# Scores of the first 128 keys in three high/low passes, with their parts in free slots of the gated outputs

## The chip, the cores and the metric

The kernel runs on one NeuronCore of a Trainium2 chip. TensorE multiplies matrices into the eight banks of PSUM; VectorE, ScalarE (called ACT in the profile) and GpSimd (POOL) work beside it; the DMA transfers are issued from SyncE (SP). Each engine works through its own instructions in order, and they hand over to each other by semaphores. The metric is the device time of one execution in microseconds, the median of the runs.

## The reference

One decoder layer on x of 4 batches, 256 tokens and 256 channels, in float32: gated linear attention with a decay in 16 heads of 128, then attention over a context, then a layer of 16 routed and 2 shared experts. The change touches the first part alone:

```python
q, k = silu(conv(h @ Wq)), silu(conv(h @ Wk))      # causal convolution of 4 taps
q, k = layernorm(q) * qn_w + qn_b, layernorm(k) * kn_w + kn_b   # per head of 128
for t in range(256):                               # for each batch and head
    S = (1 - beta[t]) * S + beta[t] * outer(v[t], k[t])
    o[t] = S @ q[t]
x = x + (o * silu(h @ Wg)) @ Wo
```

The kernel computes the recurrence of a head as a masked product: for each batch, the scores k q^T of all pairs of tokens, times a matrix of decays, times beta v.

## The kernel before

All of x stays in SBUF, 1024 tokens in 8 tiles of 128. The transposed, normalised input is kept twice, as a high part (xT_hi, in the reduced type fp32r) and a low part (xT_lo, what is left). A product in three passes, mm3 (L1344 to L1348), adds high by low, low by high and high by high, each a matmul on fp32r data; mm (L1341) is one matmul on plain float32.

The attention is a pipeline over the 16 heads. step(g, k) handles head 4g + k on each engine, and beside it the early parts of heads k + 1 and k + 2. The order is written out by hand in each engine's step. What follows is the order in TensorE's step (L1582 to L1618) before the change:

- values_unit twice (values of a later pair of heads, two units of 12 mm3 passes);
- to_features(0) to (3) (L1479): transposes of the normalised q (chunks 0, 1) and k (chunks 2, 3), with project_out of an earlier pair of heads and the gate's projection, project_in(k+1, 2, ...), between them;
- to_tokens(k+1) in four chunks (L1465): transposes after the convolution. Between them stand the q projection of head k + 2 in chunks 0 and 1 (project_in what = 0, L1445) and the scores;
- scores(g, k, b) for the batches b = 0 to 3 (L1490): two plain matmuls, the first 128 keys by all 256 queries (L1497), and the other 128 keys by the last 128 queries (L1498);
- outputs(0), the k projection of head k + 2 in two chunks (what = 1), outputs(1). The chunk u of q and k waits for taps_done, the taps of chunk u - 2, since it reuses the bank that they read (L1455).

ACT's step (L754 to L785) holds: normalise (L661) of four chunks, affine (L675), which drains the transposes with the norm's weight and bias into qk, gates (L642), silu (L655), first_taps (L625) of head k + 2, gated_high (L686), the high part of the outputs of the head before, and high, the high part of the weights. POOL's step (L491 to L507) holds the low parts: gated_low (L461), split_low for the weights, low_values or low_projection, and last_tap (L453), the last tap of the convolution. VectorE's step (L1132 to L1162) holds: the norm's factors (L1055), gated_out (L1087), taps (L1062, L1070), the scan of the decays (L1036, L1042), add_unit, head_stats (L1045, L1051) of head k + 1, and decayed (L1078, L1084), scores times decay, for each batch as it comes. Its order from the scores on: decayed(0), decayed(1), head_stats(2), decayed(2), taps(k+2, 0), decayed(3), head_stats(3), taps(k+2, 1), gated_out(0).

The scores go through two banks (c_ring); t_drained counts ACT's drains, c_drained VectorE's. gated_hi and gated_lo have four slots of 1024 columns, one for each head of a group. Head 15 is written out on its own (ACT L795 to L800, TensorE L1628 to L1648), heads 14 and 15 have no head k + 2.

Of the kernel before, what the change touches and what calls it, by code (L numbers as in the profile page):

```python
# [25 lines left out]
P = 128  # L26
# [4 lines left out]
N = 512  # L31
# [95 lines left out]
def decoder_layer(nc, x_in, ctx_in, xw_in, xb_in, wb_in, bb_in, w_in, prm_in, wv_in, wo_in,  # L127
# [5 lines left out]
    with ctx:  # L133
# [104 lines left out]

        bank = [ctx.enter_context(nc.psum_tensor(f"bank{i}", [P, N], F32)) for i in range(8)]
# [21 lines left out]
        t_full, t_drained = sem("t_full"), sem("t_drained")  # L261
        c_full, c_drained = sem("c_full"), sem("c_drained")
# [173 lines left out]
        def _(pool):  # L436
# [40 lines left out]
            split_low(0, 1)  # L477
            last_tap(0, 0, range(2 * NCH))
# [12 lines left out]
            def step(g, k):  # L491

                pool.wait_ge(rstd_ready, units(g, k, 1, 1))
                if has(g, k - 1):
                    gated_low(*head(g, k - 1), 0)
                if has(g, k + 1):
                    last_tap(*head(g, k + 1), (1,))
                    last_tap(*head(g, k + 1), (2,))
                low_shared(g, k)
                if has(g, k + 1):  # L500
                    last_tap(*head(g, k + 1), (3,))
                if has(g, k - 1):
                    gated_low(*head(g, k - 1), 1)
                if has(g, k + 2):
                    last_tap(*head(g, k + 2), (0,))
                if has(g, k + 1):
                    split_low(*head(g, k + 3))  # L507
# [72 lines left out]
        def _(act):  # L580
# [104 lines left out]

            def gated_high(g, k, c):  # L686
# [67 lines left out]
            def step(g, k):  # L754
# [8 lines left out]
                affine(g, k, (1,))  # L763
                if has(g, k + 1):
                    silu(*head(g, k + 1), (1,))
                    gates(*head(g, k + 1), (1,))
                affine(g, k, (2,))
                affine(g, k, (3,))
                if has(g, k + 1):
# [28 lines left out]
            affine(g, k, range(2 * NCH))  # L798
# [541 lines left out]
        def _(pe):  # L1340
# [149 lines left out]
            def scores(g, k, some):  # L1490

                for b in some:

                    pe.wait_ge(t_drained, units(g, k, 8, 7 + b // BPC))
                    pe.wait_ge(c_drained, c_scores(g, k) + (b - 1))
                    q0, k0 = b * L, T + b * L
                    mm(c_ring[b % 2][:, 0:L], qk[:, k0:k0 + P], qk[:, q0:q0 + L], True, True)  # L1497
# [84 lines left out]
            def step(g, k):  # L1582
# [19 lines left out]
                if has(g, k + 1):  # L1602
                    to_tokens(*head(g, k + 1), (1,))
                scores(g, k, (0,))
# [4 lines left out]
                if has(g, k + 2):  # L1609
                    project_in(*head(g, k + 2), 0, (1,))  # L1610
                scores(g, k, (3,))
                if has(g, k + 1):
                    to_tokens(*head(g, k + 1), (3,))
                outputs(g, k, (0,))
# [218 lines left out]
```

## Time and profile before

| | |
|---|---|
| median of 3 runs | 578.58 us (578.08 to 578.64) |
| the profiled execution | 578.73 us |
| its span | 576.9 us |
| busy in the span | TensorE 96%, its weight loads 84%, VectorE 75%, ACT 69%, POOL 51% |
| granted TensorE clock | 0.997 of full speed |
| attention | to about 400 us; heads 2 to 13 take 22.9 us each |

The page lists the busy time of each engine, the waits with what ended them, and the chain of work that ended last. The timeline gives, for each instruction or merged run of equal instructions, the start, the time from the first start to the last end, the engine, the line, the operation with its operands and, in brackets, the idle time of the engine before it with what ended it. The start of the next row is often before the end of the one above, as instructions are pipelined. A plain float32 matmul shows as two records.

### The profile page before, as it was taken

To read this page: it belongs to the slowest core of one execution; us is meant where nothing else is said; L and a number is where in the kernel's file an instruction comes from. 1 tells how busy PE (TensorE), PEld (TensorE's weight loads), DVE (VectorE), ACT (ScalarE), POOL (GpSimd) and SP (SyncE) were. 2 spreads that over 40 slices of the span, in tenths; PEclk is the share of its full clock that TensorE was granted. 3 is DMA by queue.
4 is the path that set the end of the run, shared out by engine and by line. 5 is a ranking of instruction groups with operands and counts; after the bars stand their busy time and mean duration, and the time that the engine had idled before them with its cause. 6 is when DMAs were issued, how large, how long until landed. Compare 5 with 4: busy or idle time off the path is not lost.

```text
span 576.9 us, 9944 instructions
## 1 busy us (share of the span) xinstructions
PE 554.7 (96%) x3392; PEld 485.0 (84%) x3392; DVE 432.5 (75%) x1046; ACT 398.1 (69%) x782; POOL 292.7 (51%) x194
## 2 busy tenths in 40 slices
PE   4898999999999999999999999989899999999997
PEld 1597889989989999899899898878678888888887
DVE  8769989998998899889989998978956543323333
ACT  3979988979779789798797887786653334333431
POOL 2335756746666457366565673420021565556552
PEclk9999999999999999999999999999999999999999
DMA  6132032032030130230211202210020433233321
GB/s 201 31 120 84 0 120 84 1 119 83 3 120 25 59 120 2 82 107 15 84 51 70 83 1 102 82 30 2 1 56 5 164 129 98 95 129 127 94 81 73
DMA packets 18001, 42.31 MB, mean 73 GB/s; under 512 B 4736, under 2 KB 6528, under 8 KB 17952
## 3 DMA queue, kind: packets, MB, share of 16 engines
q1 hardware_dynamic: 17952, 41.69, 21.6%
q8 instruction: 27, 0.44, 0.3%
q14 instruction: 22, 0.18, 0.1%
HBM read 40.47 MB, written 1.21 MB: 72 GB/s over the span
## 4 chain that ended last, share of the span: by engine, by line
PE 85%; DVE 7%; ACT 4%; issue 1%; DMA 1%; SPq 1%; DVEq 0%; ACTq 0%
PE bank L1346 21%; PE bank L1348 20%; PE bank L1347 20%; PE bank L1342 14%; PE bank L1486 5%; PE bank L1474 4%; ACT tok L671 2%; DMA w_raw<-in_w 1%; DVE stats L1051 1%; DVE xT_lo L986 1%; DVE stats L971 1%; DVE x L1187 1%; ACT values L585 1%; DVE x L1336 0%; DVE raw L1070 0%
## 5 line engine op out<-in xcount | busy, mean ns | idle before, releaser
L1346 PE MATMUL bank<-xT_lo,w_hi 128*128 128x512 f32 x320 | 133.7, 418 | 1.9 <-DVE conv L1070 1.2
L1348 PE MATMUL bank<-xT_hi,w_hi 128*128 128x512 f32 x320 | 125.9, 394 | 0.0
L1347 PE MATMUL bank<-xT_hi,w_lo 128*128 128x512 f32 x320 | 125.3, 392 | 0.0
L464 POOL TENSOR_TENSOR gated_lo<-gated,gated_hi 128x512 fp32r<-128x512 f32 x30 | 38.8, 1293 | 116.5 <-ACT gated_hi L691 112.8
L671 ACT ACTIVATE tok<-bank,nmr,rstd 128x128 f32<-128x128 f32 x256 | 91.2, 503 | 2.0 <-DVE nmr L966 2.0
L1346 PEld LDWEIGHTS bank<-xT_lo,w_hi 128*128 128x128 f32 x320 | 60.5, 189 | 16.3 <-DVE conv L1070 3.2
L459 POOL TENSOR_TENSOR raw<-tap,raw 128x506 f32<-128x506 f32 x32 | 62.0, 1936 | 20.3 <-DVE raw L1070 16.3
L459 POOL TENSOR_TENSOR conv<-tap,conv 128x506 f32<-128x506 f32 x32 | 62.0, 1936 | 20.1 <-DVE conv L1070 20.1
L1348 PEld LDWEIGHTS bank<-xT_hi,w_hi 128*128 128x128 f32 x320 | 60.2, 188 | 13.6
L1347 PEld LDWEIGHTS bank<-xT_hi,w_lo 128*128 128x128 f32 x320 | 60.7, 190 | 9.1
L1051 DVE BATCH_NORM_STATS2 stats<-bank 128x6 f32<-128x128 f32 x256 | 56.4, 284 | 14.8 <-PE bank L1474 14.8
L1042 DVE TENSOR_TENSOR_SCAN decay<-obet,dmask 128x1536 f32<-128x1536 f32 x16 | 62.0, 3873 | 0.0
L1226 DVE TENSOR_TENSOR conv<-bank,tok 128x512 f32<-128x512 f32 x36 | 24.8, 690 | 44.2 <-PE bank L1348 44.0
L1234 DVE TENSOR_TENSOR gated_lo<-gate,gated_hi 128x512 fp32r<-128x512 f32 x32 | 24.0, 785 | 39.6 <-ACT gated_hi L849 39.6
L546 POOL TENSOR_TENSOR gate<-conv,tap 128x512 f32<-128x512 f32 x32 | 42.5, 1332 | 21.4 <-DVE conv L1226 13.2
L849 ACT ACTIVATE gated_hi<-gate 128x512 fp32r<-128x512 f32 x32 | 18.9, 628 | 48.0 <-PE bank L1348 41.0
L683 ACT ACTIVATE qk<-bank,prm 128x512 f32<-128x512 f32 x64 | 51.5, 844 | 0.0
L1070 DVE SCALAR_TENSOR_TENSOR raw<-bank,prm,raw 128x510 f32<-128x510 f32 x64 | 46.8, 743 | 5.6 <-ACT tap L639 4.5
L1342 PE MATMUL bank<-qk 128*128 128x256 f32 (+1 forms) x256 | 50.2, 329 | 0.5 <-DVE x L1103 0.3
L1070 DVE SCALAR_TENSOR_TENSOR conv<-bank,prm,conv 128x510 f32<-128x510 f32 x64 | 46.8, 743 | 3.4 <-ACT tap L639 2.3
L1342 PEld LDWEIGHTS bank<-qk 128*128 128x128 f32 x256 | 43.2, 190 | 5.7 <-issue 0.7
L1342 PE MATMUL bank<-probs,values 128*128 128x256 f32 (+1 forms) x256 | 47.0, 327 | 0.0
(184 smaller groups left out, 1398.4 us busy)
## 6 DMA issues: line engine op xcount, KB each, us to landing
obet<-obet_rows SPq DMA_DIRECT2D x16, 768.0 KB, 4.3
w_raw<-in_w SPq DMA_DIRECT2D x22, 384.0 KB, 4.8
tap<-route_rows SPq DMA_DIRECT2D x16, 512.0 KB, 4.0
w_raw<-in_w SPq DMA_DIRECT2D x12, 256.0 KB, 3.0
wv_raw<-in_wv SPq DMA_DIRECT2D x8, 256.0 KB, 4.8
wo_raw<-in_wo SPq DMA_DIRECT2D x8, 256.0 KB, 4.9
w_raw<-in_w SPq DMA_DIRECT2D x12, 128.0 KB, 2.1
x<-in_x SPq DMA_DIRECT2D x2, 512.0 KB, 4.7
```

The costliest lines, as they stand in the source:

```text
L459: nc.gpsimd.tensor_tensor(y, r, y, ALU.add).then_inc(conv_done, 1)
L464: nc.gpsimd.tensor_tensor(gated_lo[:, cc], gated[:, c * N:(c + 1) * N], gated_hi[:, cc].bitcast(F32), ALU.subtract).then_inc(gated_lo_read ...
L546: nc.gpsimd.tensor_tensor(weighted(m, c), prod[:, two(m, c)], wbc[:, s * T + c * N:s * T + (c + 1) * N], ALU.mult).then_inc(e_weighted, 1)
L671: ins = nc.scalar.activation(tok[:, t * P:(t + 1) * P], t_ring[u][:, i * P:(i + 1) * P], ACT.Identity, scale=rstd[:, t:t + 1], bias=nmr[:, ...
L683: nc.scalar.activation(qk[:, u * N:(u + 1) * N], t_ring[u][:, :], ACT.Identity, scale=prm[:, o:o + 1], bias=prm[:, o + 1:o + 2]).then_inc( ...
L1042: nc.vector.tensor_tensor_scan(decay[:, :], obet[:, :], dmask[:, :], 0.0, ALU.mult, ALU.add).then_inc(decay_ready, 1)
L1051: ins = nc.vector.bn_stats(stats[:, 6 * t:6 * t + 6], t_ring[u][:, i * P:(i + 1) * P])
L1070: ins = nc.vector.scalar_tensor_tensor(out=y, in0=r, scalar=prm[:, o + 3 - back:o + 4 - back], in1=y, op0=ALU.mult, op1=ALU.add)
L1342: return nc.tensor.matmul(o, l, r, start=start, stop=stop)
L1346: nc.tensor.matmul(o, l_hi, r_lo, start=start, stop=False, skip_group_check=loose)
L1347: nc.tensor.matmul(o, l_lo, r_hi, start=False, stop=False, skip_group_check=loose)
L1348: return nc.tensor.matmul(o, l_hi, r_hi, start=False, stop=stop, skip_group_check=loose)
```

## The change

In the scores, the product of the first 128 keys with the 256 queries is taken in three passes over high and low parts (mm3), where it was one plain product. The product of the other 128 keys stays. The parts are made for each head: split_q (1024 columns of q, in slot k of gated_hi and gated_lo) and split_k (the first 128 keys of each batch, 512 columns, in slot k + 1). ACT makes the high parts (high_q(0) after affine(1); high_k and high_q(1) after affine(3)), POOL the low ones (low_q(0), low_k, low_q(1) after last_tap(3)). The scores wait for k_lo_ready and q_lo_ready instead of t_drained. In TensorE's step the second q chunk of head k + 2 moves from between scores(2) and scores(3) to ahead of scores(0), and to_tokens(3) moves ahead of scores(3).

```diff
@@ -236,6 +236,15 @@
             return (wv_hi[:, 64:64 + 3 * D], wv_lo[:, 64:64 + 3 * D]) if n == 3 else (
                 wo_hi[:, 0:3 * D], wo_lo[:, 0:3 * D])
 
+        def split_q(hi, k):
+            return (gated_hi if hi else gated_lo)[:, k % G * T:(k % G + 1) * T]
+
+        def split_k(hi, k):
+            o = (k + 1) % G * T
+            return (gated_hi if hi else gated_lo)[:, o:o + N]
+
         bank = [ctx.enter_context(nc.psum_tensor(f"bank{i}", [P, N], F32)) for i in range(8)]
         a_ring, t_ring, c_ring = bank[0:2], bank[2:6], bank[6:8]
         e_ring, y_acc = bank[0:4], bank[4:8]
@@ -259,6 +268,8 @@
         ld_route = [sem(f"ld_route{i}") for i in range(2)]
         a_full, a_copied, gate_drained = sem("a_full"), sem("a_copied"), sem("gate_drained")
         t_full, t_drained = sem("t_full"), sem("t_drained")
+        q_hi_ready, k_hi_ready = sem("q_hi_ready"), sem("k_hi_ready")
+        q_lo_ready, k_lo_ready = sem("q_lo_ready"), sem("k_lo_ready")
         c_full, c_drained = sem("c_full"), sem("c_drained")
         w_hi_ready, w_lo_ready = sem("w_hi_ready"), sem("w_lo_ready")
         wv_hi_ready, wv_lo_ready = sem("wv_hi_ready"), sem("wv_lo_ready")
@@ -475,6 +486,20 @@
             split_low(0, 0)
             low_values(0, 0)
             split_low(0, 1)
+
+            def low_q(g, k, u):
+                pool.wait_ge(q_hi_ready, units(g, k, NCH, u + 1))
+                nc.gpsimd.tensor_tensor(split_q(False, k)[:, u * N:(u + 1) * N], qk[:, u * N:(u + 1) * N],
+                                        split_q(True, k)[:, u * N:(u + 1) * N].bitcast(F32),
+                                        ALU.subtract).then_inc(q_lo_ready, 1)
+
+            def low_k(g, k):
+                pool.wait_ge(k_hi_ready, units(g, k, 1, 1))
+                nc.gpsimd.tensor_tensor(
+                    split_k(False, k).rearrange("p (b t) -> p b t", b=B),
+                    qk[:, T:2 * T].rearrange("p (b t) -> p b t", b=B)[:, :, 0:P],
+                    split_k(True, k).bitcast(F32).rearrange("p (b t) -> p b t", b=B),
+                    ALU.subtract).then_inc(k_lo_ready, 1)
             last_tap(0, 0, range(2 * NCH))
 
             def low_shared(g, k):
@@ -499,6 +524,9 @@
                 low_shared(g, k)
                 if has(g, k + 1):
                     last_tap(*head(g, k + 1), (3,))
+                low_q(g, k, 0)
+                low_k(g, k)
+                low_q(g, k, 1)
                 if has(g, k - 1):
                     gated_low(*head(g, k - 1), 1)
                 if has(g, k + 2):
@@ -682,6 +710,17 @@
                         act.wait_ge(c_full, c_scores(g, k - 1) + B)
                     nc.scalar.activation(qk[:, u * N:(u + 1) * N], t_ring[u][:, :], ACT.Identity,
                                          scale=prm[:, o:o + 1], bias=prm[:, o + 1:o + 2]).then_inc(t_drained, 1)
+
+            def high_q(g, k, u):
+                act.wait_ge(t_drained, units(g, k, 8, 4 + u + 1))
+                nc.scalar.activation(split_q(True, k)[:, u * N:(u + 1) * N], qk[:, u * N:(u + 1) * N],
+                                     ACT.Copy).then_inc(q_hi_ready, 1)
+
+            def high_k(g, k):
+                act.wait_ge(t_drained, units(g, k, 8, 8))
+                nc.scalar.activation(split_k(True, k).rearrange("p (b t) -> p b t", b=B),
+                                     qk[:, T:2 * T].rearrange("p (b t) -> p b t", b=B)[:, :, 0:P],
+                                     ACT.Copy).then_inc(k_hi_ready, 1)
 
             def gated_high(g, k, c):
 
@@ -761,11 +800,14 @@
                 if has(g, k + 1):
                     gates(*head(g, k + 1), (0,))
                 affine(g, k, (1,))
+                high_q(g, k, 0)
                 if has(g, k + 1):
                     silu(*head(g, k + 1), (1,))
                     gates(*head(g, k + 1), (1,))
                 affine(g, k, (2,))
                 affine(g, k, (3,))
+                high_k(g, k)
+                high_q(g, k, 1)
                 if has(g, k + 1):
                     silu(*head(g, k + 1), (2,))
                     silu(*head(g, k + 1), (3,))
@@ -795,7 +837,11 @@
             g, k = NG - 1, 3
             shared_high(g, k)
             normalise(g, k, range(2 * NCH))
-            affine(g, k, range(2 * NCH))
+            affine(g, k, (0, 1))
+            high_q(g, k, 0)
+            affine(g, k, (2, 3))
+            high_k(g, k)
+            high_q(g, k, 1)
             gated_high(g, k - 1, 1)
             context_exp(range(G))
 
@@ -1491,10 +1537,13 @@
 
                 for b in some:
 
-                    pe.wait_ge(t_drained, units(g, k, 8, 7 + b // BPC))
+                    pe.wait_ge(k_lo_ready, units(g, k, 1, 1))
+                    pe.wait_ge(q_lo_ready, units(g, k, NCH, 1 + b // BPC))
                     pe.wait_ge(c_drained, c_scores(g, k) + (b - 1))
                     q0, k0 = b * L, T + b * L
-                    mm(c_ring[b % 2][:, 0:L], qk[:, k0:k0 + P], qk[:, q0:q0 + L], True, True)
+                    kk, qq = slice(b * P, (b + 1) * P), slice(q0, q0 + L)
+                    mm3(c_ring[b % 2][:, 0:L], split_k(True, k)[:, kk], split_k(False, k)[:, kk],
+                        split_q(True, k)[:, qq], split_q(False, k)[:, qq], True, True)
                     mm(c_ring[b % 2][:, L:DW], qk[:, k0 + P:k0 + L], qk[:, q0 + P:q0 + L],
                        True, True).then_inc(c_full, 1)
 
@@ -1601,16 +1650,16 @@
                     project_in(*head(g, k + 2), 0, (0,))
                 if has(g, k + 1):
                     to_tokens(*head(g, k + 1), (1,))
+                if has(g, k + 2):
+                    project_in(*head(g, k + 2), 0, (1,))
                 scores(g, k, (0,))
                 scores(g, k, (1,))
                 if has(g, k + 1):
                     to_tokens(*head(g, k + 1), (2,))
                 scores(g, k, (2,))
-                if has(g, k + 2):
-                    project_in(*head(g, k + 2), 0, (1,))
+                if has(g, k + 1):
+                    to_tokens(*head(g, k + 1), (3,))
                 scores(g, k, (3,))
-                if has(g, k + 1):
-                    to_tokens(*head(g, k + 1), (3,))
                 outputs(g, k, (0,))
                 if has(g, k + 2):
                     project_in(*head(g, k + 2), 1, (0,))
```

## Rows read from the trace of the kernel before

**Rows 1.** The page's busy time, share of the span and instructions of each engine.

```profile
PE 554.7 (96%) x3392; PEld 485.0 (84%) x3392; DVE 432.5 (75%) x1046; ACT 398.1 (69%) x782; POOL 292.7 (51%) x194
```

**Rows 2.** Busy time by stretches; columns as in the first row.

```profile
core 0: us, PE busy (x) PEld busy (x) DVE busy (x) ACT busy (x) POOL busy (x), PEclk, DMA share, GB/s
92.00:346.00 254.00, 254.00 (x1645) 229.21 (x1644) 228.28 (x541) 212.43 (x422) 153.43 (x89) 1.00 0.19 63
```

**Rows 3.** Waits, 100 to 340 us: engine, line, releaser; total us, times, longest.

```profile
PEld bank L1346 <- DVE conv L1070: 1.5, 6, 0.3
...
PEld bank L1346 <- DVE raw L1070: 1.3, 5, 0.3
```

**Rows 4.** Timeline of TensorE in one head, and the next head's to_features(3).

```profile
205.06 0.28 PE L1346 MATMUL bank<-wo_lo,gated_hi 128*128 128x256 f32 x1
...
206.49 0.60 PE L1486 MATMUL bank<-ident,tok 128*128 128x128 f32 x4
...
208.32 0.60 PE L1486 MATMUL bank<-ident,tok 128*128 128x128 f32 x4
208.76 0.60 PE L1474 MATMUL bank<-ident,conv 128*128 128x128 f32 x4
...
210.58 0.60 PE L1474 MATMUL bank<-ident,conv 128*128 128x128 f32 x4
211.01 1.47 PE L1342 MATMUL bank<-qk 128*128 128x256 f32 x8
212.32 0.60 PE L1474 MATMUL bank<-ident,conv 128*128 128x128 f32 x4
...
218.62 0.47 PE L1346 MATMUL bank<-xT_lo,w_hi 128*128 128x512 f32 x1
...
231.18 0.60 PE L1486 MATMUL bank<-ident,tok 128*128 128x128 f32 x4
```

**Rows 5.** Timeline of VectorE in the same head: scan, statistics, first products, last taps.

```profile
204.21 3.87 DVE L1042 TENSOR_TENSOR_SCAN decay<-obet,dmask 128x1536 f32<-128x1536 f32 x1
...
211.21 0.89 DVE L1051 BATCH_NORM_STATS2 stats<-bank 128x6 f32<-128x128 f32 x4 [0.33 <-PE bank L1474]
212.02 1.13 DVE L1084 TENSOR_TENSOR probs<-bank,decay 128x384 f32<-128x384 f32 x2
...
217.02 1.52 DVE L1070 SCALAR_TENSOR_TENSOR raw<-bank,prm,raw 128x510 f32<-128x510 f32 x2
218.46 0.68 DVE L1095 TENSOR_TENSOR gated<-bank,gate 128x512 f32<-128x512 f32 x1
```

**Rows 6.** Timeline of ACT in the same head: gates(1), affines, gated_high, next first tap.

```profile
208.52 0.60 ACT L652 ACTIVATE gate<-bank 128x512 f32<-128x512 f32 x1 [0.73 <-PE bank L1348]
209.01 1.45 ACT L683 ACTIVATE qk<-bank,prm 128x512 f32<-128x512 f32 x2
...
212.62 0.64 ACT L691 ACTIVATE gated_hi<-gated 128x512 fp32r<-128x512 f32 x1
215.07 0.78 ACT L637 ACTIVATE raw<-bank,prm 128x512 f32<-128x512 f32 x1 [1.81 <-issue]
```

**Rows 7.** Timeline of POOL in the same head: last_tap(3) and gated_low.

```profile
204.83 4.32 POOL L459 TENSOR_TENSOR conv<-tap,conv 128x506 f32<-128x506 f32 x1
213.34 1.30 POOL L464 TENSOR_TENSOR gated_lo<-gated,gated_hi 128x512 fp32r<-128x512 f32 x1 [4.20 <-ACT gated_hi L691]
```

**Rows 8.** Timeline of head 0: ACT's last two affines and VectorE's first products.

```profile
51.74 1.57 ACT L683 ACTIVATE qk<-bank,prm 128x512 f32<-128x512 f32 x2
...
53.80 1.13 DVE L1084 TENSOR_TENSOR probs<-bank,decay 128x384 f32<-128x384 f32 x2
```

**Rows 9.** Timeline of head 14: the same two places.

```profile
369.20 1.44 ACT L683 ACTIVATE qk<-bank,prm 128x512 f32<-128x512 f32 x2
...
371.78 1.00 DVE L1084 TENSOR_TENSOR probs<-bank,decay 128x384 f32<-128x384 f32 x2
```

**Rows 10.** Timeline of head 15: affines, scores, and VectorE's wait for them.

```profile
384.49 2.88 ACT L683 ACTIVATE qk<-bank,prm 128x512 f32<-128x512 f32 x4
...
387.01 1.47 PE L1342 MATMUL bank<-qk 128*128 128x256 f32 x8
...
387.93 1.14 DVE L1084 TENSOR_TENSOR probs<-bank,decay 128x384 f32<-128x384 f32 x2 [2.02 <-PE bank L1342]
```

More of the change, by code:

```diff
@@ L1608, in step @@
                 scores(g, k, (2,))
-                if has(g, k + 2):
-                    project_in(*head(g, k + 2), 0, (1,))
-                scores(g, k, (3,))
                 if has(g, k + 1):
                     to_tokens(*head(g, k + 1), (3,))
+                scores(g, k, (3,))
                 outputs(g, k, (0,))
```

## The prediction

> **What bounds the kernel now.** I read the page's busy shares first: TensorE is busy in 96% of the span [rows 1]. By stages it is more pointed: from 92 to 346 us, some eleven heads of the attention, TensorE is busy for 254.00 of 254.00 us at a granted clock of 1.00 [rows 2]. That looks as if only TensorE's work counted. The waits of that stage say more. Weight loads of a projection (L1346) wait for VectorE's taps (L1070), once in each head: 6 + 5 times, 2.8 us in all [rows 3]. TensorE's busy share hides this, because a matmul's modelled end reaches over a short pause. So two loops close at the same moment in each head: TensorE's own work, and a loop that goes from TensorE through VectorE's queue back to TensorE.
>
> I follow one head (step k = 2 of the third group) through four engines. to_features(3) starts on TensorE at 208.32 us [rows 4]; I call this X. The same row comes 22.86 us later in the next head, at 231.18 [rows 4]. The scores start at 211.01 (X + 2.69). VectorE starts its first product of scores and decay at 212.02, right after its statistics (211.21, 0.89 us), and from there on works without a pause: four products, two groups of statistics, two pairs of taps; the second pair starts at 217.02 (1.52 us) and ends at 218.54, and the next instruction follows at 218.46 in overlap [rows 5]. The projection chunk that needs this second pair starts on TensorE at 218.62 [rows 4], 0.08 us after it. VectorE has no slack between 212.02 and 218.54: 6.52 us of back-to-back work. Whatever delays its first product delays that chunk, and all that comes after it in TensorE's order, by as much.
>
> **The change, part by part.**
>
> Scores on TensorE. A batch now costs half of 212.32 − 211.01 = 1.31 us, 0.655 us [rows 4]. Twelve high/low matmuls of 256 columns take 206.49 − 205.06 = 1.43 us, 0.119 us each [rows 4]. The 128-column product stays; the plain 256 and 128 columns share 0.655 us as 2 to 1, so it is 0.218 us and the one replaced 0.437. New batch: 3 × 0.119 + 0.218 = 0.575 us. Gain 0.08 us, for 64 batches 5.1 us. Changes between the two kinds of matmul have no clean row; between −0.02 and +0.09 us a batch, I take 0.01.
>
> ACT gets three copies of 512 columns a head. Nearest row: gated_high (L691), 0.64 us, with some 0.52 us to the next start [rows 6]. high_q(0) stands before silu(1) and gates(1). ACT waits 0.73 us ahead of gates(1) for TensorE [rows 6], so its 0.52 us is covered; without that cover it costs 0.52 us. Then gates(1) at 208.52, the affines of both halves of the key at 209.01, ended 1.45 us later at 210.46 [rows 6]. high_k waits for the last of these: 210.50 to 211.13. high_q(1) follows to 211.65, and silu(2), silu(3) and the first taps come 1.1 us later than now. That is inside the 1.81 us that ACT waits ahead of its next first tap at 215.07 [rows 6], and it must wait less there, since the moved chunk is done sooner.
>
> POOL gets three subtractions of 512 columns; nearest row gated_low (L464), 1.30 us [rows 7]. last_tap(3) starts at 204.83 and takes 4.32 us, to 209.15 [rows 7], as it lies beside VectorE's scan (204.21, 3.87 us) [rows 5]. low_q(0) runs 209.15 to 210.45; low_k can only start after high_k, at 211.21 (gated_low follows its copy by 0.08 us: 212.62 + 0.64 against 213.34 [rows 6, 7]), and ends at 212.50; low_q(1) ends at 213.75. Queued behind it are gated_low of the head before, the next last_tap(0) and split_low. The first moves from 213.34 to about 214.5; the next waits for the taps anyway.
>
> That long last_tap has a rule behind it: the Trainium skill, SBUF — State Buffer, on the shared port pair, says that a VectorE instruction with two SBUF inputs and a GpSimd one that reads SBUF lock each other out for a whole instruction. Row and rule agree. By it the three new subtractions would be spared: the VectorE work beside them, from 209.15 to 213.75, reads at most one operand from SBUF. If they were not, low_k would cost as much as last_tap; that is the third rival.
>
> The moved chunk. A chunk of a projection takes 210.58 − 208.76 = 1.82 us less the 0.44 us of four transposes (208.32 to 208.76), 1.38 us [rows 4]. It now stands in front of the scores: TensorE is free for them at 211.01 + 1.38 = 212.40, instead of 211.01. They also wait for low_k: 212.50 and 0.05 us on. So the scores start at 212.55, X + 4.23. Nearly all of this delay would be there through the moved chunk alone; without it the scores would wait idle for as long.
>
> What is late next. From the start of scores(0) to VectorE's product: in the last head, where VectorE really waits, 387.93 − 387.01 = 0.92 us [rows 10], that is 0.655 for the batch and 0.26 on the way. New: 212.55 + 0.575 + 0.26 = 213.39, against 212.02 now. The second product must wait for its batch as well, +0.08 us. Delay of the taps: 1.37 + 0.08 = 1.45 us. TensorE gets to its projection chunk at about 218.6, ahead of the taps (then at 219.97), and stands still. What it has saved on the scores is spent waiting. From that chunk to the next X nothing has changed. Hence a head takes 22.86 + 1.45 = 24.31 us, while a chunk of a later head follows: steps 2 to 13, twelve of them. 12 × 1.45 = 17.4 us. Bounds for a head: 1.2 (TensorE free at 212.40, product 0.8 us on) and 1.9 (copy and subtraction each 0.15 to 0.2 us longer, as they read runs of 128 and wait).
>
> Heads 0 and 1. ACT is busy without a gap here, so high_q(0) isn't covered. The affines start at 51.74 and end 1.57 us later [rows 8], now at 53.83; high_k to 54.53, low_k to 55.88, scores at 55.93, product at 56.77, against 53.80 now [rows 8]: 2.97 + 0.08, 3.05 us. Head 1 repeats the pattern. 6.1 us; bounds 5.4 and 7.
>
> Head 14 has no projection chunk to move. Affines from 369.20 for 1.44 us [rows 9]; high_k to 371.33, low_k to 372.70, scores at 372.75, product at 373.6 against 371.78 [rows 9]: 1.8 us, and it reaches the last head through the factors. Bounds 1.3 and 2.5.
>
> Head 15. Four affines from 384.49 take 2.88 us [rows 10]; with high_q(0) among them they end at 387.89. high_k to 388.55, low_k to 389.9, against scores at 387.01 [rows 10]: 2.9 us. As the batches are then shorter, and the later ones wait for VectorE anyway, 2.5 us reach what follows. Bounds 2 and 3.5.
>
> The sum is 17.4 + 6.1 + 1.8 + 2.5 = 27.8 us. The stages behind (experts, from some 430 us) are untouched. Against the profiled execution, 578.73 us with a span of 576.9, that is 606.5; the median, 578.58, is 0.15 lower. I say 606, with its own range of 602 (14.4 + 5.4 + 1.3 + 2.0 = 23.1 us) to 614 (22.8 + 7 + 2.5 + 3.5 = 35.8 us).
>
> **The rivals.**
>
> 1. TensorE's own work sets the time, and the copies are covered. The twelve starts at 0.08 us after the taps would then be chance. The 5.1 us less 64 × 0.01 come through: 574. This decides if VectorE can be 1.4 us late without TensorE waiting. For it speaks the 254.00 of 254.00; against it that the wait stands in every head. The Trainium skill, Perfetto Trace Analysis, Identifying the Most-Contended Engine, has the engine with the highest occupancy optimised first; followed here it leads to this rival. Chance 0.05.
>
> 2. TensorE's work sets the time, but its wait for low_k counts: 0.15 × 12, 1.7 us in each of heads 0 and 1, 1.5 and 2.5 in the last two, less 4.5: 578.7 + 1.8 + 3.4 + 4.0 − 4.5 = 583. Chance 0.06.
>
> 3. low_k is locked out by VectorE, or it locks VectorE: 4.32 instead of 1.29 us [rows 7], 3.0 us more in each of twelve heads, 36 us: 643. The work beside it speaks against it. Chance 0.05.
>
> 4. Half of the shift is taken up: by a slack of VectorE that I don't see, or hand-overs that are shorter than I take them. 0.7 to 1.1 us a head: 592 to 601. Chance 0.12.
>
> 5. The chain is longer than worked out: copies at the 0.88 us of an affine rather than 0.64, a subtraction of four runs at 1.6, 0.6 us more a head: 613 to 618. Chance 0.14.
>
> **How the numbers follow.** The forecast has 0.58. Cases 4, 5 and the forecast hold 0.84, so the range runs from 590 to 618. Slower by over 0.2% (1.2 us, about what a measurement of this kernel can tell from no change): the forecast and rivals 2 to 5, 0.95, of which I give 0.02 to a version of rival 2 that ends at no change. Slower 0.93, same 0.02, faster 0.05.
>
> **What would show it.** In the profile after: step to step 24.3 us instead of 22.86; VectorE idle for some 1.3 us ahead of its first product of scores and decay, waiting for TensorE; TensorE idle for over 1 us a head ahead of L1346, waiting for the taps; scores starting 4.2 us after X; ACT's wait ahead of the first taps gone; POOL's new subtractions at 1.3 us. If the steps stay at 22.9 us, the loop through VectorE was not binding, and the prediction falls. If VectorE waits longer than 1.8 us, the chain of copy and subtraction was priced too low.

## The result

| | before | after |
|---|---|---|
| median | 578.56 us (578.08 to 578.64) | 608.04 us (606.92 to 608.62) |
| profiled execution, its span | 578.73, 576.9 us | 608.62, 606.8 us |
| ratio after to before | | 1.051 (95% interval 1.0495 to 1.0523) |
| TensorE busy | 554.7 us, 96% | 562.7 us, 93% |

The kernel is 5.1% slower; forecast was 606 us. Of all executions behind the numbers of this document one, of the kernel with the parts and the old order, took 3122.15 us; it is left out of that kernel's median and ratio. The page's busy time of the changed kernel, against [rows 1]:

```profile
PE 562.7 (93%) x3456; PEld 487.7 (80%) x3456; DVE 433.5 (71%) x1046; ACT 421.8 (70%) x830; POOL 353.4 (58%) x242
```

ACT got 24 us and POOL 61 us of work; VectorE's work is the same, and TensorE's busy time hardly moved. So 30 us of span are not explained by any engine's busy time. They are in the waits. Waits from 105 to 360 us of the changed kernel (engine, line, releaser; total us, times, longest); L1392 answers to L1346 and L1116 to L1070 of [rows 3]:

```profile
DVE probs L1130 <- PE bank L1388: 15.4, 11, 1.4
...
PEld bank L1392 <- DVE conv L1116: 8.8, 6, 1.5
...
PEld bank L1392 <- DVE raw L1116: 7.3, 5, 1.5
```

VectorE waits once in each head ahead of its first product of scores and decay, 1.4 us; before, that wait wasn't there. And the weight load that waited 0.25 us for VectorE's taps now waits 1.5 us.

One head of the changed kernel on TensorE (timeline; columns as in [rows 4]):

```profile
222.28 0.60 PE L1532 MATMUL bank<-ident,tok 128*128 128x128 f32 x4
...
226.51 0.38 PE L1392 MATMUL bank<-gated_lo,gated_hi 128*128 128x256 f32 x1
...
227.11 0.36 PE L1392 MATMUL bank<-gated_lo,gated_hi 128*128 128x256 f32 x1
...
234.05 0.50 PE L1392 MATMUL bank<-xT_lo,w_hi 128*128 128x512 f32 x1 [1.04 <-DVE raw L1116]
...
246.66 0.60 PE L1532 MATMUL bank<-ident,tok 128*128 128x128 f32 x4
```

The first row is X. The scores start 4.23 us after it, where they started 2.69 after it [rows 4]; a batch takes 0.60 us (226.51 to 227.11). The projection chunk that needs the last taps starts after 1.04 us of an idle TensorE. The next X is 24.38 us later, not 22.86.

VectorE in the same head, against [rows 5]:

```profile
225.18 0.89 DVE L1097 BATCH_NORM_STATS2 stats<-bank 128x6 f32<-128x128 f32 x4 [0.34 <-PE bank L1520]
227.46 1.14 DVE L1130 TENSOR_TENSOR probs<-bank,decay 128x384 f32<-128x384 f32 x2 [1.40 <-PE bank L1388]
...
232.48 1.51 DVE L1116 SCALAR_TENSOR_TENSOR raw<-bank,prm,raw 128x510 f32<-128x510 f32 x2
```

It has nothing to do for 1.40 us, then works without a pause until the taps end at 233.99, 6.53 us after the first product, as before (6.52).

ACT and POOL, the chain ahead of the scores, against [rows 6, 7]:

```profile
222.48 0.60 ACT L680 ACTIVATE gate<-bank 128x512 f32<-128x512 f32 x1 [0.19 <-PE bank L1394]
222.97 1.45 ACT L711 ACTIVATE qk<-bank,prm 128x512 f32<-128x512 f32 x2
224.45 0.63 ACT L721 ACTIVATE gated_hi<-qk 128x512 fp32r<-128x512 f32 x1
```

```profile
218.79 4.32 POOL L470 TENSOR_TENSOR conv<-tap,conv 128x506 f32<-128x506 f32 x1
223.08 1.28 POOL L492 TENSOR_TENSOR gated_lo<-qk,gated_hi 128x512 fp32r<-128x512 f32 x1
225.16 1.30 POOL L498 TENSOR_TENSOR gated_lo<-qk,gated_hi 128x512 fp32r<-128x512 f32 x1 [0.80 <-ACT gated_hi L721]
```

The affines end at 224.42, high_k (L721) at 225.08, low_k (L498) at 226.46; the scores follow at 226.51. high_q(0) lies in what was ACT's wait ahead of the gates, 0.73 us before and 0.19 now.

Where the 29.9 us of span went, by the starts of to_features(3), X, of both profiles:

| stretch | before | after | more | forecast |
|---|---|---|---|---|
| start to X of head 0 | 50.10 | 51.72 | 1.62 | 0 |
| head 0 | 20.96 | 22.80 | 1.84 | 3.05 |
| head 1 | 22.89 | 25.92 | 3.03 | 3.05 |
| heads 2 to 13 | 274.56 | 292.49 | 17.93 | 17.4 |
| from X of head 14 on | 208.39 | 213.87 | 5.48 | 4.3 |

### The profile page after: what moved, and what is told of

It reads as the page before. It is cut to its first block, busy times and chain, and to the rows that moved or that the text cites. A ratio compares the mean times of both kernels' runs of the same rounds, so it can differ in the third digit from the quotient of the medians.

```text
span 606.8 us, 10168 instructions
## 1 busy us (share of the span) xinstructions
PE 562.7 (93%) x3456; PEld 487.7 (80%) x3456; DVE 433.5 (71%) x1046; ACT 421.8 (70%) x830; POOL 353.4 (58%) x242
## 3 DMA queue, kind: packets, MB, share of 16 engines
HBM read 40.47 MB, written 1.21 MB: 69 GB/s over the span
## 4 chain that ended last, share of the span: by engine, by line
PE 67%; DVE 20%; ACT 6%; issue 4%; DMA 1%; POOL 1%; SPq 0%; DVEq 0%; ACTq 0%
PE bank L1392 20%; PE bank L1394 18%; PE bank L1393 18%; DVE probs L1130 5%; PE bank L1388 5%; PE bank L1532 4%; DVE stats L1097 4%; DVE raw L1116 3%; DVE conv L1116 3%; ACT tok L699 2%; PE bank L1520 2%; ACT qk L711 1%; DMA xbias<-in_xb 1%; POOL gated_lo L498 1%; DVE xT_lo L1032 1%
## 5 line engine op out<-in xcount | busy, mean ns | idle before, releaser
L1392 PE MATMUL bank<-xT_lo,w_hi 128*128 128x512 f32 x320 | 134.5, 420 | 16.3 <-DVE conv L1116 8.4
L1392 PEld LDWEIGHTS bank<-xT_lo,w_hi 128*128 128x128 f32 x320 | 60.4, 189 | 34.0 <-DVE conv L1116 11.7
L470 POOL TENSOR_TENSOR raw<-tap,raw 128x506 f32<-128x506 f32 x32 | 62.0, 1937 | 23.4 <-DVE raw L1116 19.4
L1130 DVE TENSOR_TENSOR probs<-bank,decay 128x384 f32<-128x384 f32 x64 | 35.3, 551 | 31.5 <-PE bank L1388 31.2
L1280 DVE TENSOR_TENSOR gated_lo<-gate,gated_hi 128x512 fp32r<-128x512 f32 x32 | 23.6, 775 | 38.7 <-ACT gated_hi L895 38.6
L1116 DVE SCALAR_TENSOR_TENSOR raw<-bank,prm,raw 128x510 f32<-128x510 f32 x64 | 46.7, 742 | 5.6 <-ACT tap L667 4.4
L1116 DVE SCALAR_TENSOR_TENSOR conv<-bank,prm,conv 128x510 f32<-128x510 f32 x64 | 46.7, 742 | 3.4 <-ACT tap L667 2.3
L1388 PE MATMUL bank<-probs,values 128*128 128x256 f32 (+1 forms) x256 | 48.6, 333 | 0.0
L1388 PEld LDWEIGHTS bank<-probs,values 128*128 128x128 f32 x256 | 42.4, 191 | 6.1
```

What stands on the lines that cost most here:

```text
L470: nc.gpsimd.tensor_tensor(y, r, y, ALU.add).then_inc(conv_done, 1)
L1116: ins = nc.vector.scalar_tensor_tensor(out=y, in0=r, scalar=prm[:, o + 3 - back:o + 4 - back], in1=y, op0=ALU.mult, op1=ALU.add)
L1130: nc.vector.tensor_tensor(probs[:, bb_], c_ring[b % 2][:, 0:DW], decay[:, bb_], ALU.mult).then_inc(c_drained, 1)
L1388: return nc.tensor.matmul(o, l, r, start=start, stop=stop)
L1392: nc.tensor.matmul(o, l_hi, r_lo, start=start, stop=False, skip_group_check=loose)
```

## The experiments

Ratios are against runs of the kernel before on the same chip. "Heads" means the distance from X to X in the middle of the attention, 22.87 us before and 24.37 us after. In the cuts of code the guards `if has(...)` are left out, and `...` stands for other lines left out.

### The order alone

```diff
+                project_in(*head(g, k + 2), 0, (1,))
                 scores(g, k, (0,))
                 scores(g, k, (1,))
...
-                project_in(*head(g, k + 2), 0, (1,))
-                scores(g, k, (3,))
                 to_tokens(*head(g, k + 1), (3,))
+                scores(g, k, (3,))
```

> The kernel before, with TensorE's order of the changed one and nothing else (the scores stay plain and wait for t_drained). Theory (the loop through VectorE's queue binds, and whatever delays the first product of scores and decay delays the taps and the projection chunk behind them): the scores start at X + 4.1 instead of X + 2.7, the first product at about X + 5.0 instead of X + 3.7, a second product 0.13 us later still as its batch of 0.655 us is longer than a product: 1.4 us a head more, over 14 heads some 20 us: 598 (596 to 600). Rival, TensorE's own work sets the time: the same work in another order, 578.6. Rival, it is the wait for the low parts that costs, not the order: 579 to 583.

Measured: 597.79 us, ratio 1.0335 (1.0317 to 1.0354), heads of 24.26 us. The same instructions in another order cost 19.4 us, as expected (596 to 600). TensorE and VectorE of this kernel, with X at 219.55:

```profile
223.64 1.47 PE L1342 MATMUL bank<-qk 128*128 128x256 f32 x8
...
231.21 0.50 PE L1346 MATMUL bank<-xT_lo,w_hi 128*128 128x512 f32 x1 [1.02 <-DVE raw L1070]
```

```profile
224.56 1.21 DVE L1084 TENSOR_TENSOR probs<-bank,decay 128x384 f32<-128x384 f32 x2 [1.23 <-PE bank L1342]
```

Scores at X + 4.09, first product at X + 5.01, TensorE idle for 1.02 us ahead of the chunk: the pattern of the changed kernel, without its parts. Two products take 1.21 us here, 1.13 before: the second waits for its plain batch of 0.655 us. That TensorE's work alone sets the time is out.

### The parts without the order

> The changed kernel with TensorE's old order (second q chunk between scores(2) and scores(3)). Theory: the scores can't start before low_k is done, X + 4.2, whatever stands in front of them; TensorE now idles some 1.5 us ahead of them and no longer ahead of the projection chunk; heads of 24.4 us, 606 to 609, the same as the changed kernel. Rival, the moved chunk is what costs: back to 585 to 592.

The edit is the one above, undone in the changed kernel. Measured: 609.51 us (three executions, 607.65 to 611.86), ratio 1.0563 (1.0529 to 1.0596; the two medians alone give 1.054), heads of 24.32 us; expected were 606 to 609 us. TensorE of this kernel, X at 221.68:

```profile
225.88 0.39 PE L1392 MATMUL bank<-gated_lo,gated_hi 128*128 128x256 f32 x1 [1.34 <-POOL gated_lo L498]
```

The scores start at X + 4.20 here too, now after an idle wait for low_k. So each half of the change costs nearly the whole by itself, and the two don't add up: they run side by side and end 0.11 us apart (X + 4.09 and X + 4.20). Undoing the order alone would have won 0.05 us a head. That the median is 1.5 us above the changed kernel's goes with the clock: the three executions had a mean granted clock of 0.994, 0.992 and 0.986, from the shortest to the longest, and at 0.994 the changed kernel took 608.05 us against 607.65 here.

### The copies alone

The edit is to the changed kernel. The scores read q and k again, TensorE's old order is back as above, and ACT waits for the low parts in three places before it writes again what they are made from or kept in:

```diff
+                        act.wait_ge(q_lo_ready, units(g, k, NCH))
...
-                    pe.wait_ge(k_lo_ready, units(g, k, 1, 1))
-                    pe.wait_ge(q_lo_ready, units(g, k, NCH, 1 + b // BPC))
+                    pe.wait_ge(t_drained, units(g, k, 8, 7 + b // BPC))
...
-                    mm3(c_ring[b % 2][:, 0:L], split_k(True, k)[:, kk], split_k(False, k)[:, kk],
-                        split_q(True, k)[:, qq], split_q(False, k)[:, qq], True, True)
+                    mm(c_ring[b % 2][:, 0:L], qk[:, k0:k0 + P], qk[:, q0:q0 + L], True, True)
```

> The high and low parts are made as in the changed kernel, but the scores use plain q and k and wait for t_drained, in the old order; later users of the buffers wait for the low parts. Theory: three ACT copies and three POOL subtractions a head lie in idle time; only heads 0, 1 and 15, where ACT has no gap, pay about 0.5 us each: 579 to 581. Rival, ACT's or POOL's added work itself lengthens a head: with 1.6 us of ACT in 14 heads up to 600.

Measured: 581.5 us, ratio 1.0058 (1.0037 to 1.0078), heads of 22.86 us. Six more instructions a head, 27 us of ACT's time and 61 us of POOL's, cost nothing in heads 2 to 13. The stretch from head 1's X to head 2's took 24.38 us instead of 22.89, as ACT has no gap in head 1: TensorE waits 0.80 us for a silu behind the copies. The expectation had 0.5 us there, so it was 1 us too low. X of head 0 came 1.64 us later than before, which is the clock's doing (last section).

### The passes alone

```diff
-                    mm(c_ring[b % 2][:, 0:L], qk[:, k0:k0 + P], qk[:, q0:q0 + L], True, True)
+                    kk, qq = slice(b * P, (b + 1) * P), slice(q0, q0 + L)
+                    mm3(c_ring[b % 2][:, 0:L], xT_hi[:, kk], xT_lo[:, kk], xT_hi[:, qq], xT_lo[:, qq], True, True)
```

> The kernel before, with the first product of each score batch in three fp32r passes that read parts already at hand (the first tokens of xT_hi and xT_lo, so these scores are not those of q and k); no copies, no new waits, old order. It shows what the three passes alone are worth. From the changed kernel's trace a batch takes about 0.61 us instead of 0.655, so TensorE has some 0.16 us a head less to do. Theory (the loop through VectorE closes at the same time as TensorE's work): almost none of it reaches the end, 577.5 to 578.6. Rival, TensorE's work sets the time: 2.5 to 5 us less, 573.5 to 576.

Measured: 576.35 us, ratio 0.9975 (0.9961 to 0.9989), heads of 22.74 us. It fell at the edge between the two expectations, and it doesn't separate them: the shorter batches also let VectorE's second product start sooner. VectorE of this kernel, X at 208.76:

```profile
212.47 1.00 DVE L1084 TENSOR_TENSOR probs<-bank,decay 128x384 f32<-128x384 f32 x2
```

Two products took 1.13 us before [rows 5], and 1.00 here; 0.13 us, just what the head lost. What reaches the head is 0.13 / 4 = 0.03 us a batch, where the forecast had TensorE save 0.08.

### VectorE's loop from both sides

One instruction of the taps of chunk 0 left out, in the changed kernel and in the one before:

```diff
-                for back in (1, 2):
+                for back in ((1, 2) if u else (2,)):
```

> The changed kernel with one of the two VectorE tap instructions of chunk 0 left out (0.72 us a head; the convolution misses the tap of one token back in that chunk). Theory: VectorE's queue between the first product and the last taps sets the head, TensorE waits 1.04 us behind it, so all 0.72 us come back in 14 heads: 10 us less, 598, and TensorE's wait shrinks to 0.3 us. Rival, TensorE's own work sets the time: 608, no change.

Measured: 597.03 us, ratio 1.0329 (1.031 to 1.035), heads of 23.56 us. TensorE of this kernel, ahead of the projection chunk:

```profile
227.88 0.50 PE L1392 MATMUL bank<-xT_lo,w_hi 128*128 128x512 f32 x1 [0.37 <-DVE raw L1116]
```

24.37 − 23.56 = 0.81 us for 0.72 us of VectorE's work, and TensorE's wait went down from 1.04 to 0.37. The stretch from the first product to the end of the last taps is 0.79 us shorter (5.74 us in the mean of heads 2 to 12, 6.52 in the changed kernel). An engine that is busy in 71% of the span sets the time.

> The kernel before, with one of the two VectorE tap instructions of chunk 0 left out (0.72 us a head), the same edit as in the changed kernel. Theory: before, TensorE's work and VectorE's loop end within 0.1 us of each other, so taking 0.72 us off VectorE gives at most 0.1 us a head: 577 to 578.6. If VectorE alone bound it: 568.5.

Measured: 578.48 us, ratio 1.0006 (0.9996 to 1.0017), heads of 22.85 us. As expected, but not for the reason given. VectorE of this kernel:

```profile
214.54 0.74 DVE L1070 SCALAR_TENSOR_TENSOR raw<-bank,prm,raw 128x508 f32<-128x508 f32 x1
215.96 0.56 DVE L1084 TENSOR_TENSOR probs<-bank,decay 128x384 f32<-128x384 f32 x1 [0.68 <-PE bank L1342]
...
217.23 1.51 DVE L1070 SCALAR_TENSOR_TENSOR raw<-bank,prm,raw 128x510 f32<-128x510 f32 x2
```

The fourth product waited 0.68 us for its scores, and the last taps came no sooner. So this kernel doesn't test the loop; another place had to be relieved:

```diff
                 decayed(g, k, (3,))
+                taps(*head(g, k + 2), 1)
                 head_stats(*head(g, k + 1), (3,))
-                taps(*head(g, k + 2), 1)
```

> The kernel before, nothing left out, with VectorE's second pair of taps ahead of head_stats(3): the taps are done some 0.6 us sooner after X, limited by ACT's first_taps(1). The tap left out before could not test this, since the next product waited for its scores instead (0.68 us) and the last taps were as late as ever. If TensorE's work binds before, with VectorE just in time: 22.85 us a head and 577.5 to 578.6. If VectorE's loop binds: TensorE's head shrinks to what its work takes, by up to 0.15 us, 576 to 577.

Measured: 577.43 us, ratio 0.9989 (0.9975 to 1.0004), heads of 22.77 us, and TensorE had no wait left in the head looked at. So before the change VectorE's loop cost 0.1 us a head, over TensorE's own 22.77 us. In the median this can't be told from no change; the heads show it, as the expectation has it for the case that VectorE's loop binds.

> The three passes on parts at hand (these scores are not those of q and k), in the kernel before, together with VectorE's second pair of taps ahead of head_stats(3). With VectorE out of the way the passes show their whole worth on TensorE. If the passes alone gave 22.74 us a head because TensorE's work binds: the same 22.74 and 576.4 here. If they were held back by VectorE: less, down to 22.6 and 574.

Measured: 575.98 us, ratio 0.9965 (0.9949 to 0.9981), heads of 22.67 us. Against 22.77 the three passes are worth 0.10 us a head with the taps out of the way. That was the prize, and it is a third of what TensorE saves. TensorE of this kernel from scores(0) to the first pass of scores(2), and VectorE's first two products, X at 186.11:

```profile
189.17 0.38 PE L1342 MATMUL bank<-qk 128*128 128x128 f32 x2
...
189.74 0.38 PE L1342 MATMUL bank<-qk 128*128 128x128 f32 x2
189.96 0.60 PE L1474 MATMUL bank<-ident,raw 128*128 128x128 f32 x4
190.51 0.35 PE L1346 MATMUL bank<-xT_lo,xT_hi 128*128 128x256 f32 x1
```

```profile
189.82 1.01 DVE L1084 TENSOR_TENSOR probs<-bank,decay 128x384 f32<-128x384 f32 x2
```

From one plain product to the next, 189.17 to 189.74, a batch takes 0.57 us, against 0.655 before: 0.08 us less. But scores(2) starts 0.55 us after the transposes ahead of it, and 0.44 before. It writes into the bank that VectorE's first product reads (c_ring has two), that product takes 0.54 us from 189.82, and scores(2) starts 0.15 us after its end. It does so in the mean of heads 2 to 13 of every kernel with passes in the scores whose trace I measured (this one, the passes alone, the changed one, the parts with the old order, high_k last); before, TensorE came there 0.19 us after that end by itself. With the taps up, TensorE is 0.16 us ahead after scores(1), 0.05 at the start of scores(2), 0.15 after scores(3) and 0.10 at the next X, against four times 0.08. This is read from the traces; no run of its own relieved that wait.

### Can the changed kernel be given its time back?

The same move of the taps in the changed kernel, and one further (the cut is of the second):

> The changed kernel, nothing left out, with VectorE's second pair of taps ahead of head_stats(3). Theory: the four statistics (0.80 us) leave the stretch between first product and taps; 24.38 - 0.80 = 23.6 us a head, TensorE's wait ahead of the projection chunk falls from 1.04 to about 0.25 us; 14 heads, 11 us less than the changed kernel: 597. Rival, the added work as such costs the time: 608.

> The same with the taps ahead of the last product of scores and decay too (0.46 us more). Theory: VectorE is now early enough, and TensorE sets the head: 24.38 less its wait of 1.04 and some 0.1 us ahead of outputs(0) and the first chunk, 23.2 to 23.3 us, 591 to 594; what is left over the kernel before is TensorE's waits for low_k and for the products, and the uncovered starts of heads 0, 1, 14 and 15. If 24.38 falls by less than 0.9 us, another wait has come in its place.

```diff
                 taps(*head(g, k + 2), 0)
+                taps(*head(g, k + 2), 1)
                 decayed(g, k, (3,))
                 head_stats(*head(g, k + 1), (3,))
-                taps(*head(g, k + 2), 1)
```

Measured: 600.52 us (ratio 1.0397, 1.0373 to 1.0421) and 601.61 us (1.0408, 1.0385 to 1.043), both with heads of 23.92 us. Both fell short: the first was expected at 23.6 us a head and 597 us, the second at 23.2 to 23.3 and 591 to 594. The second's trace, first VectorE, then TensorE:

```profile
200.88 1.14 DVE L1130 TENSOR_TENSOR probs<-bank,decay 128x384 f32<-128x384 f32 x2 [1.40 <-PE bank L1388]
...
210.33 0.69 DVE L1141 TENSOR_TENSOR gated<-bank,gate 128x512 f32<-128x512 f32 x1
```

```profile
211.17 0.36 PE L1392 MATMUL bank<-wv_lo,xT_hi 128*128 128x256 f32 x1 [0.58 <-DVE gated L1141]
...
219.61 0.60 PE L1532 MATMUL bank<-ident,tok 128*128 128x128 f32 x4
```

The chunk no longer waits for the taps, but TensorE's second values unit waits for gated_out(1), which frees its bank and stands at the end of VectorE's queue, behind the norm's factors. From the first product VectorE works on without a pause for 9.45 us. The loop: 4.24 us from X to the scores, 0.95 to the product, 9.45 in VectorE's queue, 0.84 to the values unit, 8.44 to the next X, together 23.92. A second loop through VectorE, behind the first. Both kernels have its period, though the taps end 0.46 us sooner in the second, since the place of the taps within VectorE's queue doesn't change it. The late first product shifts all of VectorE's queue, not the taps alone.

Work can also be put into the idle time ahead of the product, ACT's first taps and VectorE's:

```diff
@@ ACT @@
                 high_k(g, k)
+                first_taps(*head(g, k + 2), (0,))
                 high_q(g, k, 1)
...
@@ VectorE @@
+                taps(*head(g, k + 2), 0)
                 decayed(g, k, (0,))
```

> The changed kernel, nothing left out, with chunk 0's taps put into VectorE's idle time ahead of the first product, and ACT's first_taps(0) ahead of high_q(1) so that they are ready there. Theory: 1.44 us of VectorE work leave the critical stretch, but the first product starts some 0.4 to 0.5 us later; about 0.9 us a head come back: 23.4 to 23.6 us a head, 594 to 598. Rival, the added work as such costs the time: 608.

Measured: 598.7 us, ratio 1.035 (1.0329 to 1.0371), heads of 23.67 us, the best of the changed versions with nothing left out, though just above what was expected (594 to 598 us, 23.4 to 23.6 a head). TensorE's wait for the taps is down to 0.19 us:

```profile
204.52 0.50 PE L1392 MATMUL bank<-xT_lo,w_hi 128*128 128x512 f32 x1 [0.19 <-DVE conv L1116]
```

### How low_k counts

```diff
-                high_k(g, k)
                 high_q(g, k, 1)
+                high_k(g, k)
```

> The changed kernel with high_q(1) ahead of high_k on ACT in all heads but the last: the high and the low part of k come 0.53 us later. Theory: low_k decides when the scores start (TensorE arrives 0.13 us sooner), and the delay passes on in full: 0.5 us in 14 heads, 7 us, 615 (613 to 617); low_q(1) then is ready only 1.25 us behind low_k as now. Rival, the moved chunk decides alone: 608 to 610.

Measured: 615.12 us, ratio 1.0644 (1.0627 to 1.0662), heads of 24.72 us. The scores of this kernel start at X + 4.60 (X at 225.12):

```profile
229.72 0.39 PE L1392 MATMUL bank<-gated_lo,gated_hi 128*128 128x256 f32 x1 [0.33 <-POOL gated_lo L498]
```

The scores start 0.37 us later than in the changed kernel and the head is 0.35 us longer: low_k decides from X + 4.1 on, and its delay passes on in full. Expected were 0.53 us; high_q(1) starts at 227.14, before the last affine has ended (227.27), and so is covered in part. That the median, 7.1 us up, met the expectation is luck. The profiled executions are 5.9 us apart: nothing up to X of head 1 (74.58 and 74.52 us), 1.0 in head 1, 4.3 in heads 2 to 13, 0.6 behind them. In head 1 the granted clock was 0.79 from 80 to 88 us, behind a wait of 1.91 us for low_k; in the changed kernel it was 1.00 there, behind one of 1.54, and in the kernel with the parts and the old order 1.00 too, behind one of 2.93. So this 1.0 us can't be put down to the delay itself.

## Why the prediction was right

**The binding loop.** The step that carried the sum, that the head is set by VectorE's stretch from the first product to the last taps, held: 6.53 us against 6.52, TensorE waiting 1.04 us at the chunk, and 0.81 us back for 0.72 taken off VectorE. That the loop was just about binding before as well, which the forecast read from [rows 3], held to 0.1 us a head (22.87 against 22.77 with the taps up).

**The start of the scores.** Forecast X + 4.23, measured X + 4.23. Each link lay where it was put: affines 1.45 us, high_k 0.63, low_k 1.30. The first product was forecast 5.07 us after X (213.39 − 208.32), and came at 5.18. Heads: forecast 24.31, measured 24.37.

**Two terms that cancel.** That the head came within 0.06 us is in part luck. From the scores to the first product it took 0.95 us, not 0.84: behind its wait the first pass of scores(0) is followed by the second after 0.22 us (226.51 to 226.73), where the forecast took the 0.12 of a run of passes. And the second product was to come another 0.08 us late, waiting for its batch; two products took 1.14 us, against 1.13 before, so it was 0.01. That 0.08 belongs to the plain batch of 0.655 us, as the kernel with the order alone shows (1.21); by the forecast's own batch of 0.575 it should have been close to nothing. One term was 0.11 too small, the other 0.07 too large.

**Covered work.** ACT's and POOL's additions cost nothing in heads 2 to 13, as forecast; the kernel with the copies alone shows it. The third rival, that POOL and VectorE lock each other out, did not happen: low_k took 1.30 us, beside statistics that read PSUM alone, while last_tap beside the scan stayed at 4.32. The Trainium skill, SBUF — State Buffer, Who interferes with whom, says that a VectorE instruction with two SBUF inputs contends with a GpSimd one that reads SBUF, and one with at most one SBUF input does not. Both rows agree.

**The worth of the passes.** The price of a batch held. In the changed kernel, with the second batch of the same head:

```profile
226.97 0.39 PE L1388 MATMUL bank<-qk 128*128 128x128 f32 x2
227.11 0.36 PE L1392 MATMUL bank<-gated_lo,gated_hi 128*128 128x256 f32 x1
227.31 0.28 PE L1393 MATMUL bank<-gated_hi,gated_lo 128*128 128x256 f32 x1
227.43 0.29 PE L1394 MATMUL bank<-gated_hi 128*128 128x256 f32 x1
227.56 0.38 PE L1388 MATMUL bank<-qk 128*128 128x128 f32 x2
```

From one plain product to the next it is 0.59 us here, 0.58 in the mean of heads 2 to 13 and 0.57 in the kernel with the passes alone, where the forecast had 0.575. The change from one kind of matmul to the other costs next to nothing in a full queue: the second pass comes 0.20 us after the first, not 0.12, but the first comes 0.14 us after the plain product of 128 columns ahead of it, and transposes come 0.22 us after such a product (227.56 to 227.78). What the forecast's rival 1 had wrong is that all of it would come through: scores(2) waits for VectorE's first product, which frees its bank, and 0.10 us a head are left. So rival 1, put at 574, would have come out at about 576. The forecast itself needs none of this, as it has TensorE wait for the taps.

**Head 0** cost 1.84 us in the profile where 3.05 was forecast, because X of head 0 came 1.62 us late while ACT's chain, which decides here, hardly moved: the first product came at 57.22 us, forecast 56.77. In the kernel with the parts and the old order, where X came at 50.14, it came at 56.88, and head 0 took 24.02 us, 3.06 more than before. The forecast's arithmetic was right for the case it assumed. From the start to X of head 1 the two kernels took 74.52 and 74.16 us, against 71.06 before.

**The tail** cost 5.48 us, forecast 4.3. The two links named held: head 14's first product 1.88 us later after its X (forecast 1.8), head 15's scores 2.93 us later after its last transposes (forecast 2.9). What was not forecast is TensorE's clock between them. From X of head 14 to X of head 15 it took 16.23 us before and 19.54 after. In three other versions of the changed kernel, where the clock stayed at 1.00 there (the tap left out, both moves of the taps), it took 18.13 us, 1.90 more than before. So some 1.4 us of the 5.5 are the clock's, and the links give 4.1. Busy time by stretches, columns as in [rows 2], of the kernel before and then of the changed one:

```profile
396.00:402.00 6.00, 5.88 (x40) 4.99 (x38) 5.62 (x23) 2.71 (x6) 0.00 (x0) 1.00 0.01 3
```

```profile
396.00:402.00 6.00, 4.88 (x28) 4.88 (x29) 2.84 (x9) 2.54 (x5) 5.31 (x4) 0.72 0.31 125
```

The granted clock was 0.72 in this stretch of the changed kernel, after TensorE had waited for low_k in head 14:

```profile
397.12 0.39 PE L1392 MATMUL bank<-gated_lo,gated_hi 128*128 128x256 f32 x1 [2.72 <-POOL gated_lo L498]
```

**The chances.** Rivals 1 and 2 are out by the order-alone kernel, rival 3 by low_k's 1.30 us, rivals 4 and 5 by the head's 24.37 us. The moved chunk and the copies were rightly seen as two delays of nearly one size, of which the later decides. What the forecast did not see is that a second loop lies behind the first, through gated_out(1): it made no difference to the time, but it caps what a mend of the first can give. Of the 2.1 us of span between the 29.9 us measured and the sum of 27.8, 1.4 are the clock in head 14.

## What to carry to other kernels

An engine busy in 96% of the span can be spared work and almost nothing be gained, and an engine at 75% can set the time: look at the small wait that comes back once in each period, follow the in-order queue of the engine it names back to the first instruction that waits in turn, and ask whether the change makes that one late. Work that is put ahead of a hand-over (a chunk in TensorE's queue, a copy and a subtraction on two other engines) costs what it delays downstream, not what it takes, and two such delays of the same hand-over don't add. When a test takes work out of a queue, check that the instruction behind it could start earlier at all. And a shorter instruction helps the next one only as far as the next one's bank is free.

## What the runs showed of the hardware

A pause of TensorE can cost more than its length, and whether it does is not settled by its length. After the 2.72 us wait of head 14 the granted clock of the changed kernel was 0.72 from 396 to 402 us, a mean over the levels of 1.2 and 2.4 GHz, and two groups of four transposes took 1.06 us each instead of 0.60. The seven kernels whose scores wait for the parts all have this wait, of 2.7 us (3.1 with high_k last). In four of their profiles the clock fell behind it: the changed kernel, the parts with the old order (0.73 in the same stretch), the first taps early (0.55 from 386 to 392 us) and high_k last (0.72 from 402 to 408). In the three others, the tap left out and both moves of the taps, it stayed at 1.00. The kernel with the order alone, which has no such wait, shows 1.00 from 396 to 402.

Early in the kernel it differs even with the same work. Up to X of head 0 the kernel before and the changed one have the same instructions on TensorE, yet the granted clock from 43 to 51 us (before, then after) was

```profile
43.00:51.00 8.00, 5.77 (x38) 4.72 (x37) 7.89 (x9) 7.57 (x20) 6.74 (x4) 1.00 0.00 1
```

```profile
43.00:51.00 8.00, 5.75 (x26) 4.52 (x25) 7.86 (x10) 7.33 (x19) 6.70 (x4) 0.79 0.00 1
```

behind the same two waits of 1.5 and 0.74 us. The kernels with the order alone, the copies alone and the tap left out of the changed kernel show 0.79 there as well, the other nine 1.00. Three of these nine have their low clock sooner, 0.79 from 27 to 35 us, behind a wait of 1.2 us that the kernel before has too, with a clock of 1.00 from 27 to 35 us (this is the kernel with the passes alone):

```profile
27.00:35.00 8.00, 7.66 (x28) 6.12 (x29) 1.98 (x5) 4.02 (x6) 2.54 (x2) 0.79 0.66 216
```

X of head 0 follows from this alone: it came at 50.1 to 50.4 us in the seven profiles without an early low clock, and at 51.5 to 52.0 in the seven with one. So the 1.6 us of the first row of the table belong to no edit. They are not all lost in the end: X of head 1 came at 74.52 us in the changed kernel and at 74.16 in the one with the parts and the old order, which has no early low clock. How much stayed can't be said exactly from one profile of each. What decides whether the clock falls was not tried.
